# Prologue of a pipelined RWKV-and-experts kernel: the first sequence's routing and eight expert tiles are put ahead of the third sequence's attention products

## The reference

```python
x = x + attn(layernorm(x))          # time-mix, k/v/r projections, a recurrence over 512 steps, times sigmoid(r), Wo
x = x + ffn(layernorm(x))
# ffn of z = layernorm(x):
xc = silu(pw_w @ depthwise_conv3(z) + pw_b);  x1 = z + xc
logits = x1 @ router_w.T + router_b;  top-2 of 8 experts, softmax over the two
ye = silu(x1 @ expert_w[e].T + expert_b)       # all 8 experts, 256 -> 256
h = rmsnorm(x1 + (sum_e rw[e] * ye[e]) @ out_w.T + out_b)
out = h + ff_up(gelu(ff_down(h)))              # hidden 64
```

## Time and profile before

| what | value |
|---|---|
| median of 3 runs | 971.12 us (970.77 to 971.91) |
| the profiled execution | 976.06 us, its span 974.3 us |
| TensorE busy | 885.0 us, 91% of the span |
| VectorE busy | 854.7 us, 88% |
| ScalarE busy | 720.0 us, 74% |
| GpSimd busy | 212.2 us, 22% |

### The profile page before, as it was taken

One profiled execution on the slowest core, in us unless ns is written; L12 is line 12 of the kernel. 1 busy time (PEld: TensorE's weight loads), 2 busy tenths in 40 slices (PEclk: granted clock), 3 DMA queues, 4 the chain that ended last, 5 costly groups with the idle time before them and its releaser, 6 DMA issues. The chain is left out here.

```text
span 974.3 us, 15789 instructions
## 1 busy us (share of the span) xinstructions
PE 885.0 (91%) x4288; PEld 482.3 (50%) x4288; DVE 854.7 (88%) x1579; ACT 720.0 (74%) x1233; POOL 212.2 (22%) x472
## 2 busy tenths in 40 slices
PE   1566999999999999999999999999999999969895
PEld 0233555555545555554555555554555555535542
DVE  4997899999999999999999999999999998947562
ACT  3748787887878787886978787786978788545642
POOL 5360402221131302222131212113130220111000
PEclk9787999999999999999999999999999999989997
DMA  6110100101010000101010010101010000100000
GB/s 211 44 43 1 44 1 1 66 1 66 0 65 0 32 32 0 65 0 65 0 65 0 0 65 0 65 0 65 0 43 22 23 23 1 44 1 22 1 22 22
DMA packets 28772, 29.66 MB, mean 30 GB/s; under 512 B 2090, under 2 KB 28484, under 8 KB 28484
## 3 DMA queue, kind: packets, MB, share of 16 engines
q1 hardware_dynamic: 28740, 29.27, 9.0%
HBM read 20.87 MB, written 8.39 MB: 30 GB/s over the span
## 5 line engine op out<-in xcount | busy, mean ns | idle before, releaser
L1287 DVE SCALAR_TENSOR_TENSOR comb<-ye,rw,comb 128x256 f32<-128x256 f32 x448 | 216.2, 483 | 24.5 <-ACT ye L714 10.5
L714 ACT ACTIVATE ye<-pe 128x512 f32<-128x512 f32 x256 | 151.5, 596 | 104.6 <-PE pe L454 87.3
L454 PE MATMUL pe<-weh,x1l 128*128 128x512 f16 x512 | 194.0, 379 | 0.0
L453 PE MATMUL pe<-wel,x1h 128*128 128x512 f16 x512 | 194.0, 379 | 0.0
L452 PE MATMUL pe<-weh,x1h 128*128 128x512 f16 x512 | 194.0, 379 | 0.0
L450 PE MATMUL pe<-brow,ones 128*128 128x512 f16 x256 | 97.3, 380 | 8.6 <-ACT ye L714 8.6
L405 POOL TENSOR_TENSOR msv<-ms,rms_eps_c 128x2 f32<-128x2 f32 x32 | 14.5, 453 | 398.7 <-ACT sq L734 398.7
L376 POOL TENSOR_TENSOR mo<-st 128x4 f32<-128x4 f32 x32 | 12.0, 376 | 332.4 <-DVE st L1091 194.5
L454 PEld LDWEIGHTS pe<-weh,x1l 128*128 128x128 f16 x512 | 50.0, 98 | 60.5
L453 PEld LDWEIGHTS pe<-wel,x1h 128*128 128x128 f16 x512 | 50.0, 98 | 60.5
L452 PEld LDWEIGHTS pe<-weh,x1h 128*128 128x128 f16 x512 | 50.0, 98 | 50.3
(11 more groups left out here) (152 smaller groups left out, 1943.9 us busy)
## 6 DMA issues: line engine op xcount, KB each, us to landing
xa<-in_x SPq DMA_DIRECT2D x16, 512.0 KB, 3.6
xres<-in_x SPq DMA_DIRECT2D x16, 512.0 KB, 4.4
out_y<-yo SPq DMA_DIRECT2D x16, 512.0 KB, 2.9
ye<-in_w_expert SPq DMA_DIRECT2D x2, 1024.0 KB, 8.0
wa<-in_w_attn SPq DMA_DIRECT2D x1, 1024.0 KB, 11.6
wpw<-in_w_pw SPq DMA_DIRECT2D x1, 256.0 KB, 11.7
wout<-in_w_out SPq DMA_DIRECT2D x1, 256.0 KB, 7.2
wdown<-in_w_down SPq DMA_DIRECT2D x2, 64.0 KB, 5.9
```

The source lines that it names most:

```text
L453: nc.tensor.matmul(dst, x1h[:, h, tok], wel[:, h, cols], start=False, stop=False)
L454: mm = nc.tensor.matmul(dst, x1l[:, h, tok], weh[:, h, cols], start=False, stop=h == H - 1)
L714: act.activation(ye[:, i % NY, :], pe[:, i % 2, :], ACT.Silu, scale=1.0 / WSCALE).then_inc(ye_ready.sem, 1)
L1287: v.scalar_tensor_tensor(out=comb[:, t, :], in0=src, scalar=rw[:, t, e:e + 1], in1=comb[:, t, :], op0=ALU.mult, op1=ALU.add).then_inc(comb ...
```

## The change

Each of the prologue's iterations is reordered so that sequence 0 goes first.

1. For n = 0, 1, 2 and for LayerNorm 2 of sequence 0, VectorE makes mean and variance itself (`moments_here`: four `bn_aggr`, two small instructions), and GpSimd does only the power and one product (`rstd_short`). Sequence 3 and later keep `rstd`.
2. `expert_parts` is split: its first half stays, the second goes behind the mixes xk and xv of sequence 0.
3. Iteration -3 (a = 0, n = 1): `stats_front` goes behind `difference_sd`; the reciprocal and the quotient of sequence 0 are taken in this iteration.
4. Iteration -2 (b = 0, a = 1, n = 2): TensorE begins with the projection of sequence 0 and puts its `turn_proj` between the v and the r product of sequence 1. VectorE takes the residual sums, both LayerNorm statistics and the convolution ahead of the recurrence of sequence 1. Then follow, in the same iteration, the pointwise product, x1, the router, the pick, eight expert tiles (0 to 7) and their weighted sums of sequence 0. Mixes xk and xv of sequence 2 now stand among these.
5. Iteration -1 (f = 0, b = 1, a = 2, n = 3): all that was done already is left out for sequence 0 (`lead`); tiles 8 to 15 remain, behind `turn_front` of sequence 3. The k product of sequence 2 waits for the logits to be read.

The transfers and SyncE's list are unchanged. Cut to the core:

```diff
@@ GpSimd
+            def rstd_short(seq, mo, dst, shift, moments, ready, used):
+                pool.wait_ge(moments.sem, moments.at(seq))
+                if on(seq - 1):
+                    pool.wait_ge(used.sem, used.at(seq - 1))
+                nc.gpsimd.tensor_tensor(dst[:], mo[:, 3], minus_half[:], ALU.pow).then_inc(ready.sem, 3)
+                pool.wait_ge(ready.sem, ready.at(seq, 3))
+                nc.gpsimd.tensor_tensor(shift[:], mo[:, 0], dst[:], ALU.mult).then_inc(ready.sem, 1)
...
-                if on(n):
+                if on_vector(b, 1):
+                    rstd_short(b, mo2, rstd2, shift2, moments2, rstd2_ready, xn2_ready)
+                if on_vector(n, 3):
+                    rstd_short(n, mo1, rstd1, shift1, moments1, rstd1_ready, xn1_ready)
+                elif on(n):
                     rstd(n, st1, mo1, pw1, rstd1, shift1, stats1, moments1, rstd1_ready, xn1_ready)
@@ TensorE
+                if first_proj:
+                    project()
                 if on(a):
...
+                        if lead:
+                            te.wait_ge(s1_ready.sem, s1_ready.at(f, half + 1))
+                            te.wait_ge(logits_read.sem, logits_read.at(f))
                         product(pk[:, half, :], wa[:, 0], half, xk, kvr_done)
...
+                if first_proj:
+                    turn_proj()
                 if on(a):
                     te.wait_ge(mixed.sem, mixed.at(a))
...
-                if on(f):
+                if on(f) and not lead:
                     experts(1, (0, 1, 2))
                 if on(n):
                     turn_front()
+                if first_proj:
+                    pointwise_lead(0)
+                    pointwise_lead(1)
+                    router(b)
+                    experts(0, seq=b)
+                    experts(1, seq=b)
                 if on(f):
-                    experts(1, (3,))
+                    if not lead:
+                        experts(1, (3,))
                     turn_combined(f, 0)
                     experts(2)
                     experts(3, (0, 1))
-                if on(b):
+                if on(b) and not first_proj:
                     turn_proj()
@@ ScalarE, iterations -4 to -2
+                    if is_first(b):
+                        copy_k()
+                        normalise_proj(range(NT))
+                        copy_v()
+                        copy_proj()
+                        first_tap()
+                        exponentials()
+                        act.preload_act_table_set("sigmoid_and_others")
+                        sigma()
                     normalise_front(range(NT))
...
+                    if is_first(a):
+                        act.preload_act_table_set("natural_log_exp_and_others")
+                        reciprocal(a)
+                    if is_first(b):
+                        act.preload_act_table_set("silu_and_others")
+                        pointwise_silu(0, b)
+                        pointwise_silu(1, b)
+                        fade(1, 0)
+                        fade(1, 1)
+                        high_x1(b)
+                        fade(2, 0)
+                        fade(2, 1)
+                        keep_x2(b)
+                        silus(0, range(NG), b)
+                        tanh_gap(b)
+                        silus(1, range(NG), b)
+                        return
@@ VectorE
+                def moments_here(seq, st, mv, mo, stats, moments, ready):
+                    dve.wait_ge(stats.sem, stats.at(seq))
+                    if on(seq - 1):
+                        dve.wait_ge(ready.sem, ready.at(seq - 1))
+                    for t in range(NT):
+                        v.bn_aggr(mv[:, t, :], st[:, t, :]).then_inc(moments.sem, 1)
+                    dve.wait_ge(moments.sem, moments.at(seq, NT))
+                    v.tensor_scalar(mo[:, 3], mv[:, :, 1], LN_EPS, None, ALU.add).then_inc(moments.sem, 1)
+                    v.tensor_scalar(mo[:, 0], mv[:, :, 0], -1.0, None, ALU.mult).then_inc(moments.sem, 2)
...
                 if on(n) and not on(f):
-                    if on(b):
-                        quotient()
+                    if is_first(n):
+                        stats_front()
+                        moments_front()
+                        expert_parts(0)
                     if on(a):
                         mix(a, 2, xr)
-                    stats_front()
-                    if is_first(n):
-                        expert_parts()
+                    if is_first(b):
+                        residual(0)
+                        residual(1)
+                        stats_proj()
+                        moments_here(b, st2, mv2, mo2, stats2, moments2, rstd2_ready)
+                        stats_front()
+                        moments_front()
                     if on(a):
                         running_maximum()
                         differences()
                         difference_sd()
-                    if on(b):
-                        residual(0)
-                        residual(1)
-                        stats_proj()
-                    if on(a):
+                    if is_first(a):
+                        stats_front()
+                        moments_front()
+                    if is_first(b):
+                        convolve(b)
+                    if is_first(b):
+                        for i in range(5):
+                            wkv_step(i)
+                        add_x1(b)
+                        wkv_step(5)
+                        low_x1(b)
+                        wkv_step(6)
+                        copy_logits(b)
+                        wkv_step(7)
+                        dve.wait_ge(logits_read.sem, logits_read.at(b))
+                        largest(0, lg, b)
+                        ranked(0, lg, b)
+                        first_of(0, b)
+                        select(0, b)
+                        second_logits(b)
+                        top_gap(b)
+                        wkv_step(8)
+                        ranked(1, lg2, b)
+                        first_of(1, b)
+                        select(1, b)
+                        wkv_step(9)
+                        mix(n, 0, xk)
+                        route_weights(b)
+                        for i in range(2 * NG):
+                            combine(b, i // NG, i % NG)
+                            if i == 3:
+                                mix(n, 1, xv)
+                        return
+                    if is_first(a):
                         for i in range(10):
                             wkv_step(i)
+                        quotient(a)
                     mix(n, 0, xk)
-                    if on(b):
-                        convolve(b)
                     mix(n, 1, xv)
+                    if is_first(n):
+                        expert_parts(1)
                     return
```

More of the change, by code:

```diff
@@ L584, in body @@
                     pointwise(1)
-                if on(b) and not on(f):
+                if on(b) and not on(f) and not first_proj:
                     project()
+                if first_proj:
+                    turn_proj()
                 if on(a):
@@ L601, in body @@
                     transpose_all(hh, t4_done)
-                if on(f) and not draining:
+                if on(f) and not draining and not lead:
                     pointwise(0)
@@ L869, in body @@
                     sigma()
-                if on(f) and not draining:
-                    act.preload_act_table_set("silu_and_others")
-                if on(f):
+                if on(f) and not lead:
                     if not draining:
+                        act.preload_act_table_set("silu_and_others")
                         pointwise_silu(0)
                         pointwise_silu(1)
-                    for h in range(H):
-                        act.wait_ge(x1_ready.sem, x1_ready.at(f, h + 1))
-                        if on(g):
-                            act.wait_ge(moe_done.sem, moe_done.at(g))
-                        act.copy(x1h[:, h, :], x1[:, h, :]).then_inc(x1h_ready.sem, 1)
+                    high_x1(f)
                 if on(g):
@@ L913, in body @@
                 if on(f):
-                    silus(1, (3,))
+                    if not lead:
+                        silus(1, (3,))
                     if on(n):
@@ L1181, in body @@
                     wkv_step(1)
-                if on(f):
-                    for h in range(H):
-                        dve.wait_ge(s1_ready.sem, s1_ready.at(f, h + 1))
-                        v.tensor_tensor(x1[:, h, :], x1[:, h, :], xt2[:, h, 2:2 + T], ALU.add).then_inc(x1_ready.sem, 1)
-                    for h in range(H):
-                        dve.wait_ge(x1_ready.sem, x1_ready.at(f, h + 1))
-                        dve.wait_ge(x1h_ready.sem, x1h_ready.at(f, h + 1))
-                        if on(g):
-                            dve.wait_ge(moe_done.sem, moe_done.at(g))
```

(12 more changed lines are left out.)

285 lines of the change are left out of this document (164 added, 121 removed).

## The result

The changed kernel takes 979.21 us (median of 4 runs, 978.47 to 980.09); the kernel before took 971.51 beside it (4 runs, 970.77 to 973.05). The ratio is 1.0070, 95% interval 1.0050 to 1.0091: slower by 0.5 to 0.9%, as forecast. The forecast time of 976.0 was 3.2 too low, inside its range.

The account below looks back on a forecast made before the run. TensorE was taken to pace steady iterations, VectorE's list and waits the prologue. Sequence 3's k product at 111.5 + 28.1 = 139.6 against 134.32, 5.3 later, made 981.4 profiled; less 4.9, 976 us, range 968 to 984.

Parts of the forecast that it names:

- The start: Opening of the prologue: k product of sequence 0 at 17.2 instead of 22.94, first scan at 25.1 instead of 28.77.
- Iteration -2: Prologue, quotient of sequence 0 to scan of sequence 2: VectorE work 48.5 plus waits 1.0 and 5.5, 55.0 us.
- Iteration -1: Prologue: scan to sequence 3's statistics 10.8, at 111.5, 8.1 late; then 28.1 to its k product, GpSimd chain uncovered.
- TensorE's pause ahead of the transposes: Iteration -1, a sign of being right: TensorE idle about 8 us before the transposes of sequence 3.
- the chain's low end of 4.0: Lower bound for sequence 3's GpSimd chain, taken as 6.0: ten instructions of 0.21 and a power of 1.88.
- rival (2): VectorE alone sets iteration -2, no waits, scan of sequence 2 at 94.2; 1.2 to 4.5 us faster, near 968; chance 0.19.
- The sum: k product of sequence 3 at 139.6 against 134.32, 5.3 us later; profiled execution 981.4, median 976.
- the 4.9 us taken off: Last step: the earlier profiled execution, 976.06, lay 4.9 above its median, 971.12, so 981.4 became 976.4.
- The uncovered chain: Iteration -1: tiles 0 to 6 no longer cover sequence 3's GpSimd chain, 6.0 us, so TensorE waits for the transposes.
- The half clock: TensorE slow after pauses: projection 5.5 instead of 3.6, transposes 1.5 instead of 1.04, tile 8 2.3 instead of 1.5.
- rival (3): Whole prologue: the two sides cancel, sequence 3's statistics near 106.2; within 1.9 us, 971; chance 0.18.
- rival (4): Worst holds: `wel` holds the first product (2.3), chain 9.6, half clock lasts (1.5); 12 to 13 us slower, 983; chance 0.11.

Follow-up runs that it names:

- e9: Changed kernel with short GpSimd chains and moments on VectorE for sequence 3's statistics and sequence 1's projection too; 974.42 us, ratio 1.0027 to the kernel before.
- e7: Changed kernel plus unread matmuls of constants (16, 8, 11 and 9) in four TensorE pauses; 975.36 us, ratio 1.0019 to the kernel before.
- e2: Kernel before with parts 1 to 3 of the change only, TensorE's order untouched; 971.40 us, ratio 0.9989 to the kernel before.
- e3: Changed kernel with only tiles 0 to 3 of sequence 0 early, tiles 4 to 7 back in iteration -1; 978.34 us, ratio 1.0051 to the kernel before.
- e11: Changed kernel without part 1, every scale and shift by the long GpSimd chain; 991.24 us, ratio 1.0187 to the kernel before.
- e8: e2 with k's mix earlier in the prologue, pointwise product ahead of r and sequence 3's statistics ahead of x1; 966.30 us, ratio 0.9933 to the kernel before.
- e12: e8 plus unread matmuls of constants in TensorE's pauses of iterations -3 and -2; 968.77 us, ratio 0.9965 to the kernel before.
- e1: Kernel before, unedited, timed against itself; 974.75 us against 972.94, ratio 1.0008.
- e5: Changed kernel with sequence 3's statistics first on VectorE in iteration -1, its normalisation right behind the exponentials on ScalarE; 981.26 us, ratio 1.0076 to the kernel before.
- e6: Changed kernel with moments on VectorE and the short GpSimd chain for sequence 3's statistics too; 977.47 us, ratio 1.0047 to the kernel before.

## Why the prediction was right, and where it was off

**The start** came 1.3 us earlier than worked out (k at 15.93, not 17.2): a set of moments took 0.66 us, not 1.0 (and not the 0.4 set beside it), and GpSimd had finished its second instruction at 8.84, hardly after `weh` began (8.74), and was not held. The later steps kept that lead: scan 23.91 (25.1), ev 32.05 (33.4), quotient 44.30 (45.7).

**Iteration -2** was 54.20 us from quotient to scan, forecast 55.0. Its waits sum to 6.51 (2.20, 3.41, 0.24, 0.66), forecast 6.5, and that is luck: the projection's was 1.2 larger, because it took 6.64 and not 5.5, that of x1 1.85 smaller, and the 0.66 of the tanh was not foreseen.

**Iteration -1** went as told: 10.71 from scan to statistics (10.8), the chain 5.8 (6.0), 28.6 from statistics to k of sequence 3 (28.1). TensorE's pause ahead of the transposes was 4.39, not 8, for 2.6 of the difference because r of sequence 2 at half clock pushed the projection of sequence 1 back to 110.65. Half clock lay over the transposes and tile 8, which took 1.97 and 2.67 where 1.5 and 2.3 were allowed. One bound was misread: the power of 1.88 us in the chain's low end of 4.0 ends with `weh` in the earlier trace rows and so seems to have been held by it; powers beside nothing took 1.01 and 1.02, so the low end is nearer 3.1 (ten of 0.21 and 1.01). Only the tail of rival (2) rests on it.

**The sum.** k of sequence 3 at 137.83 against 139.6. The term that was mis-sized is the last one, the 4.9 us taken off because the profiled execution lay that far above the median. The changed kernel's lies 0.9 above, so the loss in medians (7.7) is twice that in profiles (3.5 at that moment). Without the 4.9 the forecast for the profiled execution, 981.4, was 1.3 too high.

**The cause** was half told. The uncovered chain was named as the step on which the change fails, and e9 gives 3.9 us of its trace back by shortening it and the one behind it, which the prediction had not named. The half clock was counted in terms of 1 to 2 us; e7 gets 3.8 back, 3.0 of them in iteration -2. From the quotient of sequence 0 to k of sequence 3 the changed kernel takes 93.53 us and e2, without parts 4 and 5, 84.57 (44.32 to 128.89). Of these 9.0 us the chains' 3.9 in iteration -1 and the clock's 3.0 in iteration -2 would make 6.9 if they add; no run has both, so about 2 us stay open. In iteration -1 the two overlap (e9's transposes run at full clock too). Nor were part 4's moves taken apart beyond e3's four tiles. Rival (2) fell, since VectorE's waits were no smaller in sum; rival (3) as well. Of rival (4) little came: `wel` held no one, the chain took 5.8 and not 9.6, and half clock cost 0.8 more than allowed for.

**The shared port.** The Trainium skill (SBUF — State Buffer, Who interferes with whom) says that a VectorE instruction with two SBUF inputs contends with a GpSimd instruction that reads SBUF, and that one with at most one SBUF input does not, unless it runs in a 2-port mode, which `tensor_scalar` can enter. On GpSimd a small product took 1.19 beside a scan of two SBUF inputs (115.03), and the last one 0.20 beside `bn_stats` (116.29). In e11 the last product of the first chain took 1.05 and ended with `weh`, a `tensor_scalar` with one SBUF input (9.43 to 10.69). The first two rows agree with the page; the third does if `weh` ran in such a mode, which no row shows. The chain of 5.8 to 10.6 us is read by what VectorE does beside it.

## What to carry to other kernels

Ask of work pulled ahead not only what it waits for but what it was covering: here the tiles hid two chains of tiny instructions on GpSimd. A wait on TensorE has a second price in the product behind it, and it counts only if that product is waited for. So look first for an order that brings the inputs of such products earlier (e8), and fill pauses after that (e7 gained by it; in e12 filling one lengthened the next). And take a difference of medians from runs made side by side: one profiled execution can lie anywhere in its kernel's spread, and the median itself moved by 1.8 us between two sets of runs of one kernel (e1).

## What the runs showed of the hardware

- The same eleven 128x4 instructions on GpSimd took 3.9, 5.8, 9.5 and 10.6 us, by what VectorE did meanwhile.
- Four `bn_aggr` and two small instructions on VectorE take 0.66 us (0.38 for the four).
- The moment at which the clock rises again differs between executions of the same instructions: the pointwise product of sequence 0 took 4.27 us in the changed kernel, 5.76 in e5 and 5.73 in e6, which do nothing else up to there. In rows the clock is either 0.50 or 1.00 wherever it doesn't change within the stretch; the Trainium skill (TensorE: Matmul & The Clock Gate, Part 1) calls it binary, and the traces agree.
